# A linear-attention scan in chunks of 64 tokens in place of 128, with its state decayed on TensorE and two other products interleaved

## The reference

```python
xx = shift(xn) - xn                       # the token before
xk, xv, xr, xg = (xn + xx * maa for maa in (maa_k, maa_v, maa_r, maa_g))
r, k, v = xr @ Wr.T, xk @ Wk.T, xv @ Wv.T
g = silu(xg @ Wg.T)
w = exp(-exp(time_decay))                 # one decay for each head
# within a chunk of Q tokens, for each head:
att = (r_c @ k_c) * w_mat                 # w**(i-j-1) for i > j, u for i == j, else 0
y_c = att @ v_c + r_c @ state * w**i
state = w**Q * state + (k_c * w**(Q-1-j)) @ v_c
y = groupnorm(y) * gamma + beta
out = x + (y * g) @ Wo.T + square(relu(xn @ ternary(w_fc).T)) @ ternary(w_proj).T
```

## Time and profile before

| | |
|---|---|
| median of 3 runs | 604.94 us (603.67 to 606.50) |
| profiled execution, its time | 603.5 us |
| its span | 601.8 us |
| busy, share of the span | TensorE 76%, VectorE 57%, GpSimd 57%, ScalarE 32% |
| mean granted TensorE clock | 0.892 of full speed |
| block 0, to the last expert | 0 to 419 us |
| block 1 ahead of the scan | 434 to 511 us |
| the scan | 511 to 583 us |
| output products and last additions | 583 to 602 us |

### The profile page before, as it was taken

The page is one execution under the profiler, slowest core; times in us unless marked ns, Lnnn a source line. Parts: engine busy times, 40 slices in busy tenths (PEclk is TensorE's granted clock), DMA queues, the critical chain, the costliest instruction groups (busy, mean ns, idle before and its releaser), DMA issues.

```text
span 601.8 us, 8652 instructions
## 1 busy us (share of the span) xinstructions
PE 457.6 (76%) x2288; PEld 281.7 (47%) x2288; DVE 340.9 (57%) x931; ACT 194.5 (32%) x512; POOL 344.0 (57%) x327
## 2 busy tenths in 40 slices
PE   2840870688878887677678777989489989999977
PEld 1620430255545554444445444658334678455546
DVE  4799995144434444354343543542567548696983
ACT  1423220233424344343343343431074604021112
POOL 6057777777777777777787777752024001033443
PEclk9985795697879989999998997989789999797997
DMA  8511618266878778888787887863500000000002
GB/s 305 213 26 32 169 23 209 58 159 164 210 181 228 193 189 201 206 185 203 179 216 189 193 199 178 223 129 88 186 0 2 0 0 1 1 2 1 2 2 70
DMA packets 49984, 75.40 MB, mean 125 GB/s; under 512 B 14553, under 2 KB 31289, under 8 KB 49785
## 3 DMA queue, kind: packets, MB, share of 16 engines
q1 hardware_dynamic: 32968, 53.74, 30.1%
q0 software_dynamic: 16992, 21.38, 19.2%
HBM read 58.31 MB, written 15.99 MB: 123 GB/s over the span
## 4 chain that ended last, share of the span: by engine, by line
POOL 42%; PE 23%; issue 20%; DVE 8%; DMA 3%; ACT 3%; SPq 0%; POOLq 0%; DVEq 0%; ACTq 0%
POOL big L544 20%; PE ps L1312 14%; POOL routed L558 11%; POOL big L551 10%; PE ps L1576 4%; DVE big L1290 2%; DMA routed<-big 2%; PE ps L1592 2%; DMA big<-in_maa 1%; PE ps L1317 1%; ACT big L795 1%; DVE big L915 1%; DVE big L912 1%; DVE big L919 1%; PE ps L1586 1%
## 5 line engine op out<-in xcount | busy, mean ns | idle before, releaser
L1312 PE MATMUL ps<-big 128*128 128x352 f32 (+4 forms) x768 | 227.8, 445 | 17.7 <-ACT big L719 14.8
L1312 PEld LDWEIGHTS ps<-big 128*128 128x128 f32 (+2 forms) x768 | 147.6, 202 | 78.0 <-ACT big L719 25.4
L544 POOL DMA_INDIRECT big<-val_tab,big x128 | 125.4, 980 | 62.4 <-issue 38.7
L558 POOL DMA_INDIRECT routed<-big x64 | 104.3, 1630 | 34.1 <-issue 17.1
L1020 DVE SCALAR_TENSOR_TENSOR big<-big,ps 128x176 f32<-128x176 f32 x64 | 21.6, 337 | 104.3 <-ACT big L714 104.3
L1317 PE MATMUL ps<-cst,big 128*128 128x128 f32 x144 | 31.4, 307 | 57.7 <-DMA big<-tok_tab,big 55.6
L551 POOL DMA_INDIRECT big<-tok_tab,big x64 | 61.5, 962 | 22.6 <-issue 17.7
L1028 DVE COPY big<-ps 88x256 f32<-88x256 f32 x64 | 26.9, 420 | 67.9 <-PE ps L1404 67.3
L709 ACT ACTIVATE big<-ps 128x256 f32<-128x256 f32 x64 | 24.6, 384 | 110.5 <-PE ps L1317 108.9
L1317 PEld LDWEIGHTS ps<-cst,big 128*128 128x128 f32 x144 | 17.6, 150 | 76.9 <-DMA big<-tok_tab,big 51.9
L1312 PE MATMUL ps<-xnT,big 128*128 128x512 f32 (+1 forms) x104 | 51.4, 652 | 2.1 <-ACT xnT L646 2.1
(11 more groups left out here) (179 smaller groups left out, 617.2 us busy)
## 6 DMA issues: line engine op xcount, KB each, us to landing
big<-in_w SPq DMA_DIRECT2D x64, 352.0 KB
big<-in_w SPq DMA_DIRECT2D x64, 160.0 KB
big<-q_dram SPq DMA_DIRECT2D x144, 32.0 KB
routed<-big POOLq DMA_DIRECT2D x2, 1152.0 KB, 12.3
big<-val_tab,big POOLq DMA_INDIRECT x128, 2.3
big<-routed SPq DMA_DIRECT2D x4, 512.0 KB, 4.6
q_dram<-big SPq DMA_DIRECT2D x24, 64.0 KB
tok_tab<-xn SPq DMA_DIRECT2D x1, 1280.0 KB, 5.5
```

The costliest lines, as they stand in the source:

```text
L544: nc.gpsimd.indirect_dma_start(vals[:, group, side, c, :], None, val_tab, bass.IndirectOffsetOnAxis(ap=vidxT[:, col:col + 1], axis=0))\
L558: nc.gpsimd.indirect_dma_start(routed[e % 2], bass.IndirectOffsetOnAxis(ap=sidx[:, e:e + 1], axis=0), ye[:, e % 2, :], None, compute_op=AL ...
L1312: last = nc.tensor.matmul(o, w, m, start=(n == 0), stop=(n == len(pairs) - 1))
```

## The change

- The scan's chunk is 64 tokens (`Q1`), two to a tile. Scores of a unit are eight matmuls of 256 columns (32 rows by 64 weight columns), masked by VectorE in two instructions that each read two banks. Outputs are 32 matmuls of 64 columns (64 rows by 32 weight columns), and the state goes in by one matmul for each chunk but a batch's first.
- The state's decay is a matmul with a diagonal matrix (`wdiag`) ahead of the product of k and v, in one PSUM bank; VectorE only copies the result out, under the mask of heads (`state_copy`), into one of four buffers.
- The down products and the gate products leave their own stages. One of them ends each unit of the scan, down in even units and gate in odd ones, in bank 7, which the transposes of y use too. The down product's result is copied by ScalarE and added to x by GpSimd (`x2_add`); tanh and `gate` go with the gate product.
- The squares of the ReLU and the causal mask go to GpSimd; the mask's diagonal is set for eight heads at a time. The group norm's reciprocal root is one `ALU.pow` on GpSimd (32 columns, `group_rsqrt`); the square root on ScalarE and VectorE's five small steps behind it are gone.
- The mixture for v stands behind the decay of r on VectorE, the one for the gate behind the mask; it is written over `xnT`.
- SyncE issues the four small rows ahead of the accumulators and of `w5`; GpSimd takes the first `rsqrt` ahead of the fills.

```diff
+Q1 = 64
+NQ = S // Q1
...
-        yTs = v3(carve(2 * P), 2, P)
...
+        STATE_AT = []
+        for u in range(UNITS):
+            b, n = u // 8, u % 8 + 1
+            STATE_AT.append(7 * b + n if n < NQ - 1 else 7 if u == 7 else None)
...
             sp.wait_ge(s_lp, NG * 4)
+            sp.wait_ge(s_y, E + 1)
+            sp.dma_start(edrow, td_row.partition_broadcast(P)).then_inc(s_l1c, 16)
+            sp.dma_start(urow, u_row.partition_broadcast(P)).then_inc(s_l1c, 16)
+            sp.dma_start(edcol, td_col).then_inc(s_l1c, 16)
+            sp.dma_start(maat, maa).then_inc(s_l1c, 16)
             for i in range(2):
                 sp.wait_ge(s_sc[i], 16 * (1 + E // 2))
...
-            sp.wait_ge(s_y, E + 1)
             sp.dma_start(w5, w_rkvgo).then_inc(s_w5, 16)
-            sp.dma_start(edrow, td_row.partition_broadcast(P)).then_inc(s_l1c, 16)
-            sp.dma_start(urow, u_row.partition_broadcast(P)).then_inc(s_l1c, 16)
-            sp.dma_start(edcol, td_col).then_inc(s_l1c, 16)
-            sp.dma_start(maat, maa).then_inc(s_l1c, 16)
...
+            def rsqrt(n, half):
+                t = slice(half * TPB, (half + 1) * TPB)
+                pool.wait_ge(s_var, B * n + half + 1)
+                nc.gpsimd.tensor_tensor(rstd[:, 1, t], rstd[:, 0, t], rsm[:, 2, t], ALU.pow).then_inc(s_rstd, 1)
+            for half in range(B):
+                rsqrt(0, half)
             for i in range(2):
                 nc.gpsimd.dma_start(routed[i].rearrange("(r p) d -> p r d", p=P),
                                     zero[:, 0:D].rearrange("p (a d) -> p a d", a=1).broadcast_to([P, PAD // P, D]))\
                   .then_inc(s_sc[i], 16)
...
-            pool.wait_ge(s_wm1, 1)
-            nc.gpsimd.affine_select(out=wmask, in_=wmask, compare_op=ALU.is_ge, fill=0.0, base=-1,
-                                    pattern=[[0, H1], [1, P]], channel_multiplier=-1).then_inc(s_wmc, 1)
+            def square(i):
+                pool.wait_ge(s_relu, i + 1)
+                h = hf[:, i % FC, (i // FC) * S:(i // FC + 1) * S]
+                nc.gpsimd.tensor_tensor(h, h, h, ALU.mult).then_inc(s_sq, 1)
+            def causal(i):
+                w = wmask[:, i * HH:(i + 1) * HH, :]
+                pool.wait_ge(s_wm1[i], 1)
+                nc.gpsimd.tensor_tensor(w, w, const("causal").unsqueeze(1).broadcast_to([P, HH, Q1]), ALU.mult)\
+                  .then_inc(s_wmc, 1)
+            for i in range(4):
+                square(i)
+            causal(0)
+            square(4)
+            causal(1)
+            for i in range(FC, 2 * FC):
+                square(i)
...
+            def group_rsqrt(t):
+                pool.wait_ge(s_gv, t + 1)
+                g = [gst[:, k, (t % 4) * H1:(t % 4 + 1) * H1] for k in range(2)]
+                nc.gpsimd.tensor_tensor(g[1], g[0], gst[:, 2, 0:H1], ALU.pow).then_inc(s_gr, 1)
             def gated(t):
 
                 z = xn[:, t, 0:D]
                 y, g = heads_and(t, 1)
+                group_rsqrt(t)
...
+            def x2_add(t):
+                pool.wait_ge(s_ffo, t + 1)
+                nc.gpsimd.tensor_tensor(xs[:, t, :], ffo[:, t % 2, :], xs[:, t, :], ALU.add).then_inc(s_x2, 1)
...
+                if t >= 1:
+                    x2_add(t - 1)
                 if t >= 2:
                     centred(t - 2)
                 if t >= 3:
                     gated(t - 3)
+            x2_add(NT - 1)
...
+            def ff_copy(t):
+                act.wait_ge(s_ffd, t + 1)
+                if t >= 2:
+                    act.wait_ge(s_x2, t - 1)
+                nc.scalar.activation(ffo[:, t % 2, :], PS[7][:, 0:D], ACT.Copy).then_inc(s_ffo, 1)
+            def gate_tanh(t):
...
+                nc.scalar.activation(gn[:, t, :], PS[7][:, 0:D], ACT.Tanh, scale=0.5).then_inc(s_gt, 1)
...
+            def y_copy(t):
+                act.wait_ge(s_ynp, t + 1)
+                nc.scalar.activation(xn[:, t, 0:D], PS[7][:, 0:D], ACT.Copy).then_inc(s_yn, 1)
             for t in range(NT):
                 for f in range(2):
                     u = 2 * t + f
...
+                    (ff_copy, gate_tanh)[f](t)
+                    act.wait_ge(s_yTp, 2 * u + 2)
+                    nc.scalar.activation(yTs[:, u % 4, :, :], ps[:, 4:6, 0:Q1], ACT.Copy).then_inc(s_yT, 1)
                     if t >= 1:
...
+                        (y_copy, group_squares)[f](t - 1)
+            y_copy(NT - 1)
             group_squares(NT - 1)
...
+            def diagonal(i):
+                dve.wait_ge(s_wmc, i // 2 + 1)
+                h = slice(8 * i, 8 * i + 8)
+                link(nc.vector.tensor_tensor(udiag, const("diag").unsqueeze(1).broadcast_to([P, 8, Q1]),
+                                             urow[:, h].unsqueeze(2).broadcast_to([P, 8, Q1]), ALU.mult))
+                link(nc.vector.tensor_tensor(wmask[:, h, :], wmask[:, h, :], udiag, ALU.add))
...
+            mixture(3)
+            def gate(t):
                 dve.wait_ge(s_gt, t + 1)
-                nc.vector.scalar_tensor_tensor(gn[:, t, :], gn[:, t, :], 1.0, PS[t % 4][:, 0:D], ALU.add, ALU.mult)\
+                nc.vector.scalar_tensor_tensor(gn[:, t, :], gn[:, t, :], 1.0, PS[7][:, 0:D], ALU.add, ALU.mult)\
                   .then_inc(s_g, 1)
 
...
+            def state_copy(k):
+                b, n = divmod(k, NQ - 1)
+                dve.wait_ge(s_kvp, k + 1)
+                nc.vector.tensor_tensor(state[:, (NQ * b + n + 1) % 4, :, :],
+                                        PS[6][:, 0:2 * P].rearrange("p (f n) -> p f n", f=2),
+                                        const("heads").unsqueeze(1).broadcast_to([P, 2, P]), ALU.mult)\
+                  .then_inc(s_st, 1)
...
+            norm_stages = (group_means, group_variances)
+            def masked(u, k):
+                a = 2 * u + k
+                dve.wait_ge(s_a1p, 4 * a + 4)
+                if a >= 8:
+                    dve.wait_ge(s_yTp, 2 * (a // 2 - 3))
+                h = HH * (u % 2) + 8 * k
+                nc.vector.tensor_tensor(aring[:, a % 8, :].rearrange("p (q n) -> p q n", q=2),
+                                        ps[:, 2 * k:2 * k + 2, 0:4 * Q1],
+                                        wmask[:, h:h + 8, :].rearrange("p (q h) n -> p q (h n)", q=2),
+                                        ALU.mult).then_inc(s_a1, 1)
+            state_copy(0)
             for u in range(UNITS):
...
                 for q in range(4):
...
+                    if q % 2 == 0:
+                        masked(u, q // 2)
+                    elif q == 1:
+                        if STATE_AT[u - 1:u] and STATE_AT[u - 1] is not None:
+                            state_copy(STATE_AT[u - 1])
+                        if u >= 2 and u % 2 == 0:
+                            gate(u // 2 - 1)
...
+            def ff_down(t):
+                pe.wait_ge(s_sq, FC * (1 + t // TPB))
+                if t >= 1:
+                    pe.wait_ge(s_g, t)
+                product(PS[7][:, 0:D], [(hf[:, c, tok(t)], w_pj1[:, c, :]) for c in range(FC)]).then_inc(s_ffd, 1)
+            def gate_product(t):
+                pe.wait_ge(s_mix, 4)
+                pe.wait_ge(s_yn, t) if t else pe.wait_ge(s_ffo, 1)
+                product(PS[7][:, 0:D], [(mixed(3, c, tok(t)), w5[:, 3, c, :]) for c in range(DC)]).then_inc(s_gp, 1)
+            def chunk(t, c):
+                return slice(t * P + c * Q1, t * P + (c + 1) * Q1)
+            def scores(u, k):
                 t, f = divmod(u, 2)
...
+                if u:
+                    pe.wait_ge(s_a1, 2 * (u - 1) + k + 1)
+                for q in (2 * k, 2 * k + 1):
                     rows = slice(RG * q, RG * (q + 1))
...
+                    for c in range(2):
+                        nc.tensor.matmul(PS[q][c * Q1:(c + 1) * Q1, 0:4 * Q1], kT[rows, f, chunk(t, c)],
+                                         rhead[rows, f, :, chunk(t, c)], start=True, stop=True).then_inc(s_a1p, 1)
 
             def outputs(u):
                 t, f = divmod(u, 2)
                 b, g = divmod(t, TPB)
...
+                if u >= 1:
+                    pe.wait_ge(s_yT, u)
+                for c in range(2):
+                    n = 2 * g + c
+                    if n:
+                        pe.wait_ge(s_st, 7 * b + n)
+                        nc.tensor.matmul(PS[4 + c][:, 0:Q1], state[:, (NQ * b + n) % 4, f, :], rw[:, f, chunk(t, c)],
+                                         start=True, stop=False, skip_group_check=True)
+                pe.wait_ge(s_a1, 2 * u + 2)
+                pe.wait_ge(s_vd, t + 3)
                 for h in range(4):
...
+                    for c in range(2):
+                        rows = slice(c * Q1, (c + 1) * Q1)
+                        for q in range(4):
+                            at = (q % 2 * 4 + h) * Q1
+                            last = nc.tensor.matmul(PS[4 + c][32 * q:32 * q + 32, 0:Q1],
+                                                    vpr[t % 2][rows, 4 * f + q, 32 * h:32 * h + 32],
```

(33 more changed lines are left out.)

233 lines of the change are left out of this document (66 added, 167 removed).

## The result

The changed kernel takes 648.04 us (median of four runs, 645.6 to 649.87), the kernel before 605.72 beside it: ratio 1.0689, 95% interval 1.0623 to 1.0754. It is slower by 42 us, where 19.5 were forecast. The profiled execution took 645.6 us, span 643.8, mean granted clock 0.867 against 0.892.

What follows compares the result with a forecast made beforehand. VectorE bounds the scan, TensorE the projections. First outputs at 489.0, TensorE's 94.3 us and waits of 15.6, 1.1 and 3.5 reach 603.5; tail 15.2 gives 618.7, time 623.0, or 624 by the median; range 610 to 636, wide 594 to 650.

Steps and rivals of the forecast that it cites:

- the dear power: Rival: GpSimd's power goes by columns, up to 8.4 us for 32; time 643 us; chance 0.08.
- the cheap packed products: Rival in the scan: packed products run eight at once, 24.5 us less over 16 units; time 597; chance 0.24.
- I take 2.0, near the row: Group norm on GpSimd: one power of 32 columns priced at 2.0 us, between 1.05 and 8.4; three in series in the tail.
- the 15.2 itself: Tail, last y transposes to last addition: 15.2 us, 16.1 before, losing sqrt and five small operations but gaining GpSimd's powers.
- the room on GpSimd: Scan: placing v, x2, centring and four gating steps take 5.1 of 15.4 us a tile, leaving GpSimd room.
- My sum has no such term: Scan: the sum charges nothing for a falling clock, though the change leaves TensorE 2.6 us idle in nearly every tile.
- The rival of the clock: Rival: half clock in a third of the scan after TensorE's idle time costs 15 to 20 us; time 642; chance 0.10.
- outputs at 1.8: Scan: a unit's outputs, 32 products of 64 columns on TensorE, priced at 1.8 us, 3.6 a tile.
- the waits (2.15 for 2.6): Scan: TensorE idles 2.6 us ahead of second scores in six tiles, waiting through squares and variance sum for the second mask.
- the forecast's own sign, outputs under 1.0: Scan: a unit's outputs in 1.8 us would show the forecast; under 1.0 would prove packed products run eight at once.
- the first rival: Scan: packed products run eight at once, outputs 0.85 and scores 0.57 us a unit; time 597; chance 0.24.

Runs made afterwards that it cites:

- masks-first kernel: The changed kernel with both masks of a unit first on VectorE, then state copy, gate and the norm's steps; ratio 1.014 to the kernel before.

## Why the prediction was wrong

The direction was right and every wait was where the forecast put it. The median of 648.04 lies in the wide range of 594 to 650, but outside the forecast's own 610 to 636. The time was 24 us short, 22.5 of it on the profiled last addition (641.2 for 618.7): 4.8 before the first outputs, 3.9 in the scan, 13.9 in the tail. Three of the rivals held at once, at least in part, where the forecast gave each a chance for itself: the clock, the dear power, and the cheap packed products.

*The step that failed in the tail: "I take 2.0, near the row".* The power is 5.44 us for 32 columns, inside the bounds of 1.05 and 8.4 and nearer the dear end. Three in series make 10.3 of the 13.9. The rest lies in the 15.2 itself: with the power at 0.25 the tail took 14.6, so three at 2.0 would have made some 20 (an estimate from that kernel) and the forecast too low at its own price. Centring and four gating steps stand between the powers on the same engine. TensorE's last eight records are slow too, 3.62 us behind a wait of 7.27, where before they took 1.89. The working said itself that two of 4 columns can't tell fixed from growing, and then took the value near the cheap bound. In the scan, the room on GpSimd that I named was there: with the power nearly free the scan is no shorter.

*The step that failed in the scan: "My sum has no such term".* The clock cost 20.2 us, shown by the masks-first kernel, in which the same work is busy for that much less. The rival of the clock had the right place and size ("15 to 20"), but I made it a rival to the forecast when it follows from the forecast's own waits. The earlier trace rows had it: 0.56 after 1.2 us of idle time. I weighed against it with stretches whose waits were small.

*The term mis-sized the other way: outputs at 1.8.* They take 0.79 at full clock, 12.3 ns for a weight load and product, half of the 26.7 ns at twice the columns; scores 0.62 for 0.8. By the forecast's own sign, outputs under 1.0, the first rival was right on the products' price. Its reason, eight at once, isn't shown: a product's rows were halved together with its moving columns, so the runs don't separate the two, and at half clock a pair takes 17.4 ns, not twice 12.3. The outputs are thus 16 us less than forecast over 16 units, 3 more from the scores and 2.7 from the waits (2.15 for 2.6); down, gate and y transposes took some 4 more. The other waits were 1.3 longer, 1.0 of it the last y transposes' wait for the gate. Together some 16.5 less, against 20 more for the clock: the scan's 118.4 for 114.5 looks like a good forecast and is two errors that nearly cancel, which is luck. The Trainium skill's price by weight columns (TensorE: Matmul & The Clock Gate, LDWEIGHTS (loading the stationary operand)) and its overhead of 60 cycles (TensorEngine Tiling (Array Packing), Instruction Overhead) both gave 1.6 to 1.7 here, as estimates; the row has 0.79.

*Before the scan.* The gain at the start was 1.25 us and held through the expert stage; at the seam 1.9 in all, for the accumulators now land later and the additions end 0.8 after before's. TensorE's two sets of up products then took 10.65 and 10.55 us at granted clocks of 0.85 and 0.84, before 9.86 and 8.85 at 0.90 and 1.00, and the projections start at 461.26, not 458.0. The wait for k's scalings and the mixture came as forecast: v starts at 480.49 for 477.2, no later than the projections already were. v itself then took 8.83 us, at a granted clock of 0.81, where 6.9 was forecast.

*Right:* state product 1.28 (forecast 1.25), the wait's place and chain, the y transposes' 0.56 seven times, VectorE at 28% of the scan.

Was the change itself bad? With the root and the masks' order repaired it is 0.5% faster than before, and with two products moved into a gap 1.6%. With all the dense products taken out of the scan again the kernel is at 1.027; that the clock alone makes this difference isn't shown.

## What to carry to other kernels

Price a wait on TensorE with what the clock does behind it: look in the profile for one stretch with a wait of that length and read the granted clock after it, then charge the following work at that level. Here waits of one length, 1.02 us, took the clock down in some tiles and not in others, so work out the time both ways and keep both as bounds. Before moving an operation to another engine, price its copies in the tail, where nothing covers them, by the dear bound if the rows have only a smaller shape. When one engine is full and its work is cut, read again whose queue order now holds the others: here 34 us lay in the place of a mask behind a sum.
